# A chunked linear attention on one core: where evictions, gate steps and the last norm stand in the order of the engines

## The reference, cut to what matters

```
q = elu(x @ Wq + bq) + 1;  k = elu(x @ Wk + bk) + 1;  v = x @ Wv + bv      # x: 4 batches x 1024 x 128, 16 heads of 8
for each position i:  s += k_i (outer) v_i;  z += k_i;  values_i = (q_i @ s) / (q_i . z + 1e-6)
x = layernorm(x + values @ Wo + bo)
ss, sd = sigmoid(x @ Ws), sigmoid(x @ Wd)    # second layer's gates: 8 heads x 5 experts, the top 3 of 5 kept
```

## Time and profile before

| | us |
|---|---|
| median of 3 runs (lowest, highest) | 1871.56 (1870.95, 1872.44) |
| the profiled execution | 1867.74 |
| its span | 1865.9 |
| TensorE busy, share | 1684.3, 90% |
| VectorE busy, share | 1137.7, 61% |
| ScalarE busy, share | 1256.8, 67% |
| GpSimd busy, share | 866.2, 46% |

### The profile page before, as it was taken

One profiled execution on the slowest core, in us unless ns is written; L12 is line 12 of the kernel. 1 busy time (PEld: TensorE's weight loads), 2 busy tenths in 40 slices (PEclk: granted clock), 3 DMA queues, 4 the chain that ended last, 5 costly groups with the idle time before them and its releaser, 6 DMA issues. The chain is left out here.

```text
span 1865.9 us, 29217 instructions
## 1 busy us (share of the span) xinstructions
PE 1684.3 (90%) x10754; PEld 893.4 (48%) x10754; DVE 1137.7 (61%) x1948; ACT 1256.8 (67%) x2427; POOL 866.2 (46%) x575
## 2 busy tenths in 40 slices
PE   8888479999999999999999999779999999898975
PEld 4555356555565555655555555324233333332354
DVE  4666697997779886798876667431414223120196
ACT  4344115676776577675667676578899999999823
POOL 3355116787776688756787577850000000000033
PEclk9999699999999999999999999889999999999988
DMA  3000131221211121111112120230221312201001
GB/s 81 2 12 2 49 107 48 83 78 52 66 55 44 33 66 54 44 54 44 54 45 66 33 66 12 57 124 24 68 91 51 108 46 69 83 32 38 1 6 42
DMA packets 38790, 97.55 MB, mean 52 GB/s; under 512 B 5040, under 2 KB 16496, under 8 KB 38512
## 3 DMA queue, kind: packets, MB, share of 16 engines
q1 hardware_dynamic: 38640, 95.59, 16.5%
HBM read 49.96 MB, written 28.84 MB: 42 GB/s over the span
## 5 line engine op out<-in xcount | busy, mean ns | idle before, releaser
L1078 POOL TENSOR_TENSOR b_psum<-b_psum,b_probs 128x1024 f32<-128x1024 f32 x192 | 462.2, 2407 | 221.2 <-ACT b_probs L1220 214.9
L2511 ACT ACTIVATE c_probs<-banks 128x1024 f32<-128x1024 f32 x512 | 483.6, 1029 | 37.2 <-PE banks L2560 21.6
L1220 ACT ACTIVATE b_probs<-banks 128x1024 f32<-128x1024 f32 x256 | 255.5, 1020 | 231.1 <-PE banks L1360 230.3
L1325 PE MATMUL banks<-b_w,b_xh 128*128 128x480 f32 x1024 | 354.2, 398 | 33.2 <-issue 12.5
L1570 DVE TENSOR_TENSOR b_gated<-banks,b_g 128x480 f32<-128x480 f32 x512 | 310.6, 653 | 110.3 <-PE banks L1325 100.2
L1586 DVE TENSOR_REDUCE b_tok<-b_gated 128x192 f32<-128x960 f32 x256 | 281.5, 1138 | 0.5
L1189 ACT ACTIVATE b_share<-b_o,b_picked 128x64 f32<-128x64 f32 x1080 | 268.9, 340 | 1.7 <-DVE b_o L1611 1.7
L1395 PE MATMUL banks<-b_probs,b_tok 128*64 128x512 f32 x1024 | 252.1, 613 | 2.6 <-ACT b_probs L1220 2.6
L2574 PE MATMUL banks<-c_probs,c_vg 128*32 128x512 f32 x2048 | 249.7, 605 | 3.0 <-DVEq L2625 2.6
L1325 PEld LDWEIGHTS banks<-b_w,b_xh 128*128 128x128 f32 x1024 | 194.4, 190 | 116.5 <-issue 58.6
L1360 PE MATMUL banks<-b_qq,b_kk 64*128 64x512 f32 x1536 | 232.2, 426 | 5.0 <-DVE b_gated L1570 4.3
(11 more groups left out here) (265 smaller groups left out, 1814.3 us busy)
## 6 DMA issues: line engine op xcount, KB each, us to landing
b_w<-b_split_w SPq DMA_DIRECT2D x24, 960.0 KB, 4.7
b_kk<-b_kk SPq DMA_DIRECT2D x64, 256.0 KB, 3.7
c_heads<-c_split SPq DMA_DIRECT2D x24, 512.0 KB
c_keys<-c_heads SPq DMA_DIRECT2D x16, 512.0 KB, 3.8
c_queries<-c_heads SPq DMA_DIRECT2D x16, 512.0 KB, 4.7
b_split_w<-b_w SPq DMA_DIRECT2D x8, 960.0 KB, 6.1
b_raw_w<-in_L_ffn_W SPq DMA_DIRECT2D x8, 480.0 KB, 4.2
c_heads<-c_split SPq DMA_DIRECT2D x8, 384.0 KB
```

The source lines that it names most:

```text
L1078: nc.gpsimd.tensor_tensor(psum[:, par, :], prev, probs[:, i % 4, :], ALU.add).then_inc(psum_rdy, 1)
L1220: nc.scalar.activation(probs[:, i % 4, :], score_b[i % 2], ACT.Exp).then_inc(exp_rdy, 1)
L1325: last = nc.tensor.matmul(proj_b[u % WAYS][:, 0:HALF_W], a[:, x_of % 2, t * P:(t + 1) * P], w[:, par, part, j, :], start=(i == 0), stop=(i ...
L2511: nc.scalar.activation(probs[:, step % 4, c, :, :], unit_b[u % NU], ACT.Exp, scale=float(HD) ** -0.5).then_inc(exp_rdy, 1)
```

## The change

Nothing is computed otherwise; instructions change place, engine or size:

- `zero_beats` clears the diagonal alone, and stands at GpSimd's step 3 of the last batch instead of step 5.
- The second gates' piece of the last batch stands in (3, late), turn_share in (4, early).
- ScalarE: `keep_apart(b + 1, 0)` at step 4 instead of 5; `finish_norm(b - 1)` in halves at steps 5 and 6 instead of whole at 6. GpSimd: `inverse_roots(b - 1)` at step 4 instead of 5.
- VectorE: at step 0 `add_residual` ahead of the masks and `take_values` right behind them, ahead of `keep_state`; at step 6 `take_values` right behind the masks; the norm's sums one step earlier; `split_low` at step 3 of the last batch; 14 instead of 8 pieces of the gates inside the steps.
- The last batch's norm goes by the same three functions as the others.

```diff
-        self.nc.gpsimd.memset(self.beats[:, :, :, :], 0.0).then_inc(self.clear, 1)
+        own = self.beats[:, :, :, :].rearrange("p c a b -> p c (a b)")[:, :, 0:self.E * self.E:self.E + 1]
+        self.nc.gpsimd.memset(own, 0.0).then_inc(self.clear, 1)
...
-                instead = {(1, 1): [("turn_next", b, 0)], (2, 1): [("turn_next", b, 1)], (3, 0): [("gates", b, 0)], (4, 0): [("gates", b, 1)]}
+                instead = {(1, 1): [("turn_next", b, 0)], (2, 1): [("turn_next", b, 1)], (3, 0): [("gates", b, 0)], (3, 1): [("gates", b, 1)], (4, 0): [("turn_share", b, 0)]}
...
-                    if c == 5 and b:
+                    if c == 4 and b:
                         inverse_roots(b - 1)
...
-                    if c == 5 and b + 1 == B:
+                    if c == 3 and b + 1 == B:
                         pool.wait_ge(qk_rdy, 4 * B)
                         front.zero_beats()
+            inverse_roots(B - 1)
...
-                    if b + 1 < B and c in (5, 7):
+                    if b + 1 < B and c in (4, 7):
                         keep_apart(b + 1, c // 7)
...
-                    if c == 6 and b:
-                        finish_norm(b - 1)
+                    if c in (5, 6) and b:
+                        finish_norm(b - 1, c - 5)
+            for half in range(2):
+                finish_norm(B - 1, half)
...
+                    if c == 0 and b:
+                        add_residual(b - 1, 0)
                     if n + 1 < CHUNKS:
                         mask_scores(n + 1)
+                    if c == 0:
+                        take_values(b, 1)
+                    if c == 6 and b + 1 < B:
+                        take_values(b + 1, 0)
                     if c < NT - 1:
                         keep_state(n)
-                    if c == 0:
-                        if b:
-                            add_residual(b - 1, 0)
-                            values(b - 1, 1)
-                        take_values(b, 1)
+                    if c == 0 and b:
+                        values(b - 1, 1)
...
                     if c >= 4 and b == B - 1:
-                        next(gates)
-                        next(gates)
+                        for _ in range((3, 3, 4, 4)[c - 4]):
+                            next(gates)
             values(B - 1, 1)
-            for _ in range(6):
-                next(gates)
             add_residual(B - 1, 0)
             next(gates)
-            next(gates)
-            dve.wait_ge(newton, NEWTON_STEPS * (B - 1))
             add_residual(B - 1, 1)
-            dve.wait_ge(*reads(index["project", B - 1, 1]))
-            st = Steps(dve, norm_steps)
-            layer_norm(nc, st, y, out[:, (B - 1) * NT:B * NT, :], stats, mv, rs, tmp)
-            st.settle()
+            norm = moment_parts(B - 1)
+            for _ in norm:
+                pass
             for _ in gates:
                 pass
```

More of the change, by code:

```diff
@@ L353, in linear_into @@
         taken, masked_last = map(sem, ("taken", "masked_last"))
-        share_rdy, vals_rdy, xb_rdy, moments, newton, normed, norm_steps = map(sem, ("share", "vals", "xb", "moments", "newton", "normed", "norm_steps"))
+        share_rdy, vals_rdy, xb_rdy, moments, newton, normed = map(sem, ("share", "vals", "xb", "moments", "newton", "normed"))
         MASKED = NG - 1
@@ L558, in take_scores, with finish_norm @@
                 nc.scalar.copy(weights[:, n % 2, MASKED, :], ps[:, MASKED, :]).then_inc(taken, 1)
-            def finish_norm(b):
+            def finish_norm(b, half):
                 act.wait_ge(newton, NEWTON_STEPS * (b + 1))
-                for t in range(NT):
+                for t in range(4 * half, 4 * half + 4):
                     nc.scalar.activation(out[:, b * NT + t, :], y[:, t, :], ACT.Identity, bias=shift[:, t:t + 1], scale=rs[:, t:t + 1]).then_inc(normed, 1)
@@ L829, in _ @@
                     n = b * NT + c
+                    if c == 0 and b:
+                        add_residual(b - 1, 0)
                     if n + 1 < CHUNKS:
                         mask_scores(n + 1)
+                    if c == 0:
+                        take_values(b, 1)
+                    if c == 6 and b + 1 < B:
+                        take_values(b + 1, 0)
                     if c < NT - 1:
                         keep_state(n)
-                    if c == 0:
-                        if b:
-                            add_residual(b - 1, 0)
-                            values(b - 1, 1)
-                        take_values(b, 1)
+                    if c == 0 and b:
+                        values(b - 1, 1)
                     if c == 1 and b:
                         add_residual(b - 1, 1)
+                        norm = moment_parts(b - 1)
+                        next(norm)
                     if c == 2:
                         shares(b)
[L843 to L846, removed]
+                    if c in (2, 3) and b:
                         next(norm)
@@ L851, in _ @@
                         values(b, 0)
-                        if b + 1 < B:
-                            take_values(b + 1, 0)
                     if c == 7 and b + 1 < B:
                         running_sum(b + 1)
+                    if c == 3 and b == B - 1:
+                        front.split_low(dve, 0)
                     if c == 4 and b == B - 1:
-                        front.split_low(dve, 0)
                         dve.wait_ge(*reads(index["gates", b, 1]))
```

## The result

The changed kernel takes 1841.73 us (median of 4, 1838.54 to 1843.81), the kernel before 1871.26 (4 runs): a ratio of 0.9842, 95% interval 0.9825 to 0.9859, so 29.5 us less. Forecast were 1845.3 us, with a range of 1838 to 1857, and a gain of 26.3 us. The profiled executions differ by 26.7 us (1867.74 and 1841.05). The changed kernel's span is 1839.2 us; from the first projection of the second layer on (199.37 us now, 227.37 before) it is 1639.8 where it was 1638.5. Thirteen profiles of this study, whose instructions are the same from there on, have 1634.2 to 1639.8. A few us of a whole time can therefore not be given to an edit; I measure the edits inside the first stage.

The account below looks back on a forecast made before the run. Bound seen in the first stage: waits at three batch ends and one stage end, the rest full. Savings of 19.1 + 7.2 = 26.3 us take the median from 1871.56 to 1845.3 us, range 1838 to 1857.

Parts of the forecast that it names:

- the batch ends: First stage, ends of three batches: shorter waits of TensorE save 5.6, 7.2 and 6.3 us, together 19.1.
- the stage end: End of the first stage, last batch: clearing wait gone and gate steps beside the last norm, 7.2 us saved.
- the spreading of queries: Batch end, ScalarE: spreading activations at step 4 delay the next keys' exps, so the first spreading starts 1.35 us later.
- The value eviction behind the masks: Third batch's end, VectorE: values evicted by 150.3 instead of 152.0, so TensorE's 2.92 us wait before the second spreading goes.
- The key copy still 1.3 us late: Third batch's end, ScalarE: key copy done at 155.8, projection at 155.9 instead of 158.84, a wait of 1.3 us left.
- The clearing, 8.96 us: Last batch, GpSimd: clearing of b_beats at step 3 is hidden unless over 5 us; VectorE's wait was 8.96.
- GpSimd held by the gate steps: Last norm: VectorE's left gate steps lengthen GpSimd's chain by zero to 2.05 us; 1.1 taken.
- Rival B: Last norm: GpSimd shut out in full, 1.0 us more, and again beside the new split and gates: 1847.5; chance 0.15.
- Rival A: Batch ends: same waits under another name, ScalarE's list decides, each gives 3 instead of 6.4 us: 1855; chance 0.13.
- C: First stage: nearly all waits go, exps not delayed, clock stays up, 27 + 8 us: 1836; chance 0.07.
- D: Batch ends: changed order doesn't reach the waits, value eviction was not what TensorE waited for: 1871; chance 0.03.
- E: Every step: VectorE's operations with two SBUF inputs meet GpSimd's mask, costing 64 us: slower, 1909; chance 0.02.

Follow-up runs that it names:

- the early weights: The changed kernel with the two weight blocks' high and low parts made at steps 2 and 3 instead of 6: 1839.0 us, one run.
- the version that beats both: The changed kernel with queries' spreading back at step 5, old order of gate pieces and split, last residuals ahead of remaining gate pieces: 1825.44 us.

## Why the prediction was right

It was right as a whole and in its two terms: 19.1 us for the batch ends, measured 20.9 (18.8 against the periods of a profile that has no edit there); 7.2 for the stage end, measured 7.8. The 29.5 us between the medians are 3 more than forecast, within what whole times of one kernel differ by here. The main waits were settled by runs that moved one thing: VectorE's evictions alone and the clearing alone. The forecast had the cost of two moves in its terms (the spreading of queries, 1.35 us a batch, and the split ahead of the masks, 1.8 us), but not that they give less than they cost: taken back, the early spreading gives 3.4 us, and the split with the gates' new order 1.5. Point by point:

- *The value eviction behind the masks*: as worked out. The second spreading waits for nothing. The run with VectorE's moves alone carries 19.1 of the 20.9 us.
- *The spreading of queries costs 1.35 us*: 1.28 more of waiting for a_expo, and 0.9 to 1.3 us back when undone.
- *The key copy still 1.3 us late*: 1.13. The step was right, the weight laid on it not: the early weights show that VectorE's list, with the scan in it, ends no earlier if the key copy does. The forecast had followed that list as well. It let VectorE's values end at 160.8 and the next scores start at 161.8; in the trace, set on the same start, they are at 160.5 and 161.3. So it still came out right.
- *Batch ends at 16 to 17.7 us*: from the first spreading, which itself starts 1.3 us later, to the scores the trace has 15.1, 15.8 and 15.8 us, a little under the 16 to 18 that was named as the sign. The forecast's per batch saving was 5.6, 7.2 and 6.3; the periods give 6.3, 7.8 and 6.9. In the third batch the 0.6 is the 0.5 us by which the scores come earlier than forecast. How near the other two are is in part luck: against the unedited periods of the clearing's run the savings are 5.0, 6.9 and 6.9, so the first was forecast too high and the third too low.
- *The clearing, 8.96 us*: fully gone, as forecast. But the sum booked 8.3 less 1.1 for all edits of the last batch and so hid that one of them is worth 9.6 and the others cost 2. The delay of the masks by 1.8 us was in the sum; that it was avoidable was not seen.
- *The last residual at 206.5, the statistics done at 210.0, the last activation at 217.3, or 218.4 with GpSimd held*: with the last denominators set on the same start the trace has 206.7, 210.3 and 218.1.
- *The norm over three engines gains nothing itself*: right, 0.5 us against VectorE alone, which is not more than E differs by itself.
- *GpSimd held by the gate steps, 1.1 us, between 0 and 2.05*: 0.56 (4.50 against 3.94), mis-sized by half. Rival B, the full length of all five operations, did not come.
- Rival A, the same waits under another name, did not come for the change, but is exactly what came for the early weights. Of C the clock at its upper level came in the profile of the result, the rest did not; D and E did not come.

## What to carry to other kernels

Ask of each moved item which wait it ends, and move it for that wait alone: here VectorE's moves and one clearing give nearly all of the gain (18.3 and 10.1 us of 29.5 when done apart). Of the other moves, the norm in halves with its earlier steps gained some 5 us, and the early spreading of the queries and the new order of the gates lost about as much. A total that comes out right can hold losers: undo the parts one by one when the sum is in. And on an in-order engine put what another engine waits for (the last residuals) ahead of work that nobody waits for (the gate pieces): this, together with the old order of the gates, was worth 6 us more.

## What the runs showed of the hardware

VectorE and GpSimd hold each other, and which operation does it can be read from steps of known length. A Newton step of GpSimd takes 0.20 us. Beside VectorE's reductions it does so too (from 190.15 above, while they ran from 189.97 to 191.84); beside the operations on the gates it took 0.28 to 0.33; beside a comparison of two gate operands in the version that beats both, 0.84:

```profile
180.19 0.84 POOL L445 TENSOR_SCALAR a_tmp<-a_tmp 128x8 f32<-128x8 f32 x1
```

The wait is the rest of the one operation that VectorE has begun, not the sum of those behind it. In the changed kernel's last norm each held step ends about 0.05 us behind an operation of VectorE, as this step at 192.79 behind this copy at 192.75 (a line of each engine's timeline):

```profile
192.42 0.33 DVE L306 COPY b_picked<-b_mask 128x320 f32<-128x320 f32 x1
192.51 0.28 POOL L443 TENSOR_TENSOR a_tmp<-a_rs 128x8 f32<-128x8 f32 x1
```

GpSimd's steps slip in between, and five held steps cost 0.56 us where the five operations last 2.07 (191.88 to 193.95). The Trainium skill ("SBUF — State Buffer", "Who interferes with whom") says that VectorE's reductions never contend with GpSimd, that an instruction with two inputs in SBUF does with a GpSimd instruction that reads SBUF, and that one in a two-port mode does too, whoever comes second waiting for the whole of the other. The trace agrees (0.20 us beside the reductions, 0.28 to 0.84 beside the others), and adds that for a chain of short steps the price can be far below the length of what runs beside it. It works the other way round as well: a TENSOR_SCALAR of 8 elements on VectorE, 0.16 us where no clearing stands beside it (the run with the clearing alone), took 1.82 in the changed kernel while GpSimd cleared beats:

```profile
160.91 1.82 DVE L817 TENSOR_SCALAR a_tmp<-a_mv 128x8 f32<-128x8 f32 x1
```

The clearing itself shrank less than its elements: 640 elements a partition, each six behind the last, take 1.81 us, 3200 in a row 2.77.
